# The dense sums of a node group, added in four steps at four successive tiles

## What is computed

```python
h = jnp.einsum('ni,rio->rno', X, W)                  # 4 relations
msg = h[etype, src] * inv_deg[:, None]
agg = jax.ops.segment_sum(msg, dst, num_segments=X.shape[0])
out = agg + X @ root + bias
out = (out - mu) * jax.lax.rsqrt(var + EPS) * gamma + beta
out = jax.nn.elu(out)
return out + X
```

## Time and profile before

| what | value |
|---|---|
| median of 3 runs | 5862.45 us (5860.99 to 5867.11) |
| span of the profiled execution | 5905.4 us |
| PE busy | 4806.4 us, 81% |
| DVE busy | 3711.0 us, 63% |
| POOL busy | 3267.9 us, 55% |
| ACT busy | 1418.0 us, 24% |

### The profile page before, as it was taken

How to read it: one execution, slowest core, us unless ns; L and a number is a source line. 1 busy time by engine, 2 the same in 40 slices (tenths; PEclk the granted TensorE clock), 3 DMA queues, 4 the chain that set the end, 5 groups by cost and what they waited for, 6 DMA issues and landing times.

```text
span 5905.4 us, 80081 instructions
## 1 busy us (share of the span) xinstructions
PE 4806.4 (81%) x20415; PEld 3355.2 (57%) x20415; DVE 3711.0 (63%) x9969; ACT 1418.0 (24%) x3629; POOL 3267.9 (55%) x3256
## 2 busy tenths in 40 slices
PE   5878876777888887888887888887888888777776
PEld 4544432345666665666664666665666665556555
DVE  7998885565666664555554555555556555566665
ACT  1046653213555551111111111111111111011011
POOL 0058871003666664666664666665666664666664
PEclk8999998999999998999998999998999998888888
DMA  1000016312555555555555555555555555444444
GB/s 49 1 1 1 1 21 228 143 61 89 159 156 161 162 158 170 161 157 155 159 157 150 162 156 159 159 155 161 155 158 155 159 159 152 144 143 145 143 140 126
DMA packets 398886, 772.61 MB, mean 131 GB/s; under 512 B 77327, under 2 KB 166113, under 8 KB 398424
## 3 DMA queue, kind: packets, MB, share of 16 engines
q0 software_dynamic: 150720, 386.19, 24.2%
q1 hardware_dynamic: 246824, 380.53, 19.2%
q10 hardware_dynamic: 1008, 1.84, 0.1%
HBM read 652.04 MB, written 115.89 MB: 130 GB/s over the span
## 4 chain that ended last, share of the span: by engine, by line
PE 65%; issue 13%; DVE 12%; another core or an unknown queue 5%; ACT 2%; DVEq 2%; DMA 1%; ACTq 0%; SPq 0%
PE psum L736 24%; PE psum L758 23%; PE psum L690 5%; PE psum L807 3%; DVE arena L1429 3%; PE psum L840 2%; PE psum L793 2%; DVE arena L1571 2%; DVE arena L1303 2%; DVE arena L1290 2%; PE psum L700 1%; DVE arena L1238 1%; PE psum L622 1%; DVE emat L1409 1%
## 5 line engine op out<-in xcount | busy, mean ns | idle before, releaser
L584 POOL DMA_INDIRECT msg<-h_table,g_rel x1880 | 1795.6, 955 | 1088.5 <-issue 419.9
L1429 DVE TENSOR_TENSOR arena<-arena,psum 128x256 f32 x2940 | 1224.7, 417 | 1434.8 <-PE psum L758 970.4
L758 PE MATMUL psum<-msg,emat 128*128 128x256 f32 x4704 | 1519.7, 413 | 547.7 <-issue 323.1
L758 PEld LDWEIGHTS psum<-msg,emat 128*128 128x128 f32 x4704 | 892.9, 202 | 1021.7 <-issue 795.6
L1409 DVE TENSOR_SCALAR emat<-iota,node,weight 128x128 f32<-128x128 f32 x2352 | 862.9, 368 | 139.4 <-issue 58.8
L736 PE MATMUL psum<-arena,emat 128*128 128x256 f32 x3200 | 908.1, 405 | 6.3 <-issue 6.1
L584 POOL DMA_INDIRECT msg<-h_table,g_src x472 | 457.0, 968 | 726.3 <-PE psum L758 591.0
L736 PEld LDWEIGHTS psum<-arena,emat 128*128 128x128 f32 x3200 | 647.5, 204 | 134.0 <-issue 35.5
L566 POOL DMA_INDIRECT placed_rows<-leaving,idx x300 | 439.6, 1465 | 423.3 <-issue 416.7
L584 POOL DMA_INDIRECT hout<-h_table,g_rel x472 | 451.3, 956 | 275.4 <-issue 110.2
L793 PE MATMUL psum<-arena,emat 125*128 125x453 f16 x2000 | 448.0, 358 | 85.9 <-DVE arena L1303 85.9
(11 more groups left out here) (253 smaller groups left out, 5331.1 us busy)
## 6 DMA issues: line engine op xcount, KB each, us to landing
emat<-count_blocks SPq DMA_DIRECT2D x496, 256.0 KB
more_blocks<-count_blocks SPq DMA_DIRECT2D x372, 256.0 KB
count_blocks<-emat SPq DMA_DIRECT2D x200, 256.0 KB
h_table<-hout SPq DMA_DIRECT2D x100, 512.0 KB
msg<-h_table,g_rel POOLq DMA_INDIRECT x1880
arena<-h_table SPq DMA_DIRECT2D x24, 512.0 KB
msg<-h_table,g_src POOLq DMA_INDIRECT x472
hout<-h_table,g_rel POOLq DMA_INDIRECT x472
```

Of the source, the lines that this page charges most:

```text
L584: pool.indirect_dma_start(out=slots[n % RING], out_offset=None, in_=table[:, :], in_offset=bass.IndirectOffsetOnAxis(ap=rows[:, t:t + 1], ...
L758: pe.matmul(agg_ps[n % NPS][:, 0:D], emat[:, n % BODY, :], slots[n % RING], start=True, stop=True).then_inc(s_mm, 1)
L1429: dve.tensor_tensor(a, a, agg_ps[n % NPS][:, 0:D], ALU.add).then_inc(s_acc, 1)
```

## The change

In passes 1 to 4 the four additions of dense sums of a window no longer follow one another. Relation r has the key d - DA + r, so the four stand behind the additions of tiles d-6, d-5, d-4 and d-3. Each addition of the tile behind a step waits for that step (`s_dstep`, and `s_dense` behind the last one). In pass 0 the one addition stays where it is, and the wait for it moves from right behind it to just ahead of the next tile's addition. PE, ACT, POOL and SP execute the same instructions in the same order as before.

```diff
+            dense_step_at = {done_at[j] - DA + r: (j, r) for j in range(NW) for r in range(R)}
+
             def add_tiles(q, work):
...
+                    if t in dense_step_at:
+                        j, r = dense_step_at[t]
+                        if q == 0 and r == 0 or r == R - 1:
+                            dve.wait_ge(s_dense, q * NW + j + 1)
+                        elif q:
+                            dve.wait_ge(s_dstep, ((q - 1) * NW + j) * (R - 1) + r + 1)
                     dve.wait_ge(s_mm, MM0 + n + 1)
...
-            def dense_added(q, j):
+            def dense_begun(q, j):
                 n, v = q * NW + j, window_at(mybir.EngineType.DVE, j)
-                a = cols(acc, v * D, D)
                 dve.wait_ge(s_used, (n + 1) * K)
-                dve.wait_ge(s_acc, ACC0 + q * NT + done_at[j] - DA)
                 if q == 0:
...
+            def dense_added(q, j, r, v):
+                n, a = q * NW + j, cols(acc, v * D, D)
+                dve.wait_ge(s_acc, ACC0 + q * NT + done_at[j] - DA + r)
+                added = dve.scalar_tensor_tensor(
+                    a, dense_ps[r // 2][:, r % 2 * D:(r % 2 + 1) * D],
+                    cols(inv, v + r * NW, 1), a, ALU.mult, ALU.add)
+                if r < R - 1:
+                    added.then_inc(s_dstep, 1)
                 else:
-                    for r in range(R):
...
-                dve.wait_ge(s_dense, n + 1)
+                    added.then_inc(s_dense, 1)
...
                 for j in range(NW):
-                    steps[done_at[j] - DA] = lambda j=j: dense_added(q, j)
+                    for r in range(R if q else 1):
+                        steps[done_at[j] - DA + r] = lambda j=j, r=r: dense_step(j, r)
```

More of the change, by code:

```diff
@@ L1558, in window_work @@
                 return work
-            def dense_added(q, j):
+            def dense_begun(q, j):
                 n, v = q * NW + j, window_at(mybir.EngineType.DVE, j)
-                a = cols(acc, v * D, D)
                 dve.wait_ge(s_used, (n + 1) * K)
-                dve.wait_ge(s_acc, ACC0 + q * NT + done_at[j] - DA)
                 if q == 0:
+                    a = cols(acc, v * D, D)
+                    dve.wait_ge(s_acc, ACC0 + q * NT + done_at[j] - DA)
                     dve.tensor_tensor(a, a, dense_ps[0][:, 0:D], ALU.add).then_inc(s_dense, 1)
-                else:
-                    for r in range(R):
[L1569 to L1574, removed]
-                dve.wait_ge(s_dense, n + 1)
+                return v
+            def dense_added(q, j, r, v):
[6 more added lines that the diff above has]
+                    added.then_inc(s_dstep, 1)
+                else:
+                    added.then_inc(s_dense, 1)
             def window_steps(q):
@@ L1588, in window_steps, with dense_step @@
                 after = sorted(window_work(q, 0, 0) if q else first_work(0, 0))
+                dense_of = {}
+                def dense_step(j, r):
+                    if r == 0:
+                        dense_of[j] = dense_begun(q, j)
+                    if q:
+                        dense_added(q, j, r, dense_of[j])
                 for j in range(NW):
-                    steps[done_at[j] - DA] = lambda j=j: dense_added(q, j)
+                    for r in range(R if q else 1):
+                        steps[done_at[j] - DA + r] = lambda j=j, r=r: dense_step(j, r)
                     for i in after:
```

## The result

The changed kernel takes 5874.02 us (median of 20 runs, 5859.51 to 5889.03), the kernel before, on the same chip, 5863.96 us (median of 20, 5856.70 to 5873.81). The ratio is 1.0018, 95% interval [1.0012, 1.0024]: about 10 us slower, just inside the 0.2% that I had called "same". I had forecast 33 us slower. The direction was right, the size three times too large.

What follows compares the result with a forecast made beforehand. No engine was full; waiting between PE and DVE was taken as the bound. Later dense products cost 43 us in passes 1 to 3, pass 4 0, 10 us given back: +33, 5862 to 5895 us, range 5800 to 5945.

Steps and rivals of the forecast that it cites:

- The stall ahead of tile d-1, up to 1.93 us earlier: PE may start tile d-1 up to 1.93 us earlier per window; taken alone worth at most 193 us.
- The dense product at 5.5 at the earliest, and 1.0 us later in half of the windows: PE's first dense product waits for the fourth step; passes 1 to 3: half the windows 1.0 later, half 0.2, 43 us.
- The late results: PE's results reach DVE later than modelled matmul ends; late case taken for half of 72 windows, start 1.0 us later.
- Pass 4 and pass 0 at nothing: Pass 4's 24 windows cost 0; in pass 0 only the wait of its one addition per window moves: nothing.
- What is given back, 10 us: Less queued on DVE behind the window's end, and PE's tiles d-1 and d done earlier: 10 us taken back.
- The clock, as before: PE's spells at the lower clock, 1.2 GHz, stay as many as before, in pass 4 too.
- DVE's own work at nothing: DVE's work grows one or two tenths of a us per window, covered by idle time: nothing; uncovered, 15 us.
- gain reaches the path: Rival: late windows start the dense product at 5.5, half their low-clock spells go; 5767 full, 5815 half; chance 0.31.
- Nothing in sum: Rival: losing and gaining windows cancel, or the four banks even it out; 5863, within 0.2%; chance 0.18.

Runs made afterwards that it cites:

- the second profile of before: The kernel before, unchanged, profiled once more because its first profiled execution was a long one: span 5856.5 us, time 5858.26 us.
- e5_one_of_four: The kernel before with only the last relation's dense addition in passes 1 to 4, the other three left out: 5848.74 us, ratio 0.9970.
- e13_bank_wait2: The changed kernel, but a window's first two dense products wait only for the second dense addition, the third for the fourth: 5911.11 us, ratio to before 0.9997.
- e15_two_and_two: Half way between the kernel before and the changed one: two dense additions behind tile d-6, two behind tile d-5; 5911.14 us, ratio to before 1.0004.
- e12_changed_again: The changed kernel, unchanged, run again on another chip: 5928.64 us, ratio to the kernel before 1.0032.
- e8_run_at_d2: The kernel before with its run of four dense additions kept whole but three tiles later, behind tile d-3: 5932.36 us, ratio 1.0122.
- e9_half_products: The kernel before without the dense products of relations 1 and 2 in passes 1 to 4, 14 per window in place of 28: 5831.59 us, ratio 0.9934.
- e10_half_gathers: The kernel before, gathering only 64 of a tile's 128 rows in passes 1 to 4: 5869.66 us, ratio 0.9997.

## Why the prediction was right in direction and wrong in size

*The stall ahead of tile d-1, up to 1.93 us earlier.* Right as to the mechanism. Summed over the 100 windows of passes 1 to 4, PE's idle time just ahead of tile d-1 fell from 168 us in the second profile of before to 48. That this is worth less than its length was expected; with it and three quarters of the additions gone `e5_one_of_four` gained 16 us, and in the two versions without a wait (`e13_bank_wait2`, `e15_two_and_two`) it is worth nothing measurable.

*The dense product at 5.5 at the earliest, and 1.0 us later in half of the windows.* Right in its place, right in sum, somewhat wrong in its parts. Over the 72 windows of passes 1 to 3, the first product started 6.19 us behind the addition of tile d-6 in the second profile of before, and 6.68 in the changed kernel: 0.49 x 72 = 35 us, where I had 43 (pass 4, which I had at nothing, adds 6). Starts beyond 7 us were 14 and became 27, so fewer windows had been late than the half I took. The three examples of the earlier trace rows came from an execution with more of them (21). The cycle of a tile and a step is 1.24 and 1.22 us where nothing is late (3407.36, 3408.60 and 3409.82 in DVE's rows above), not 1.40, so that the earliest start is 1.47 + 1.24 + 1.22 + 0.56 + 0.48 + 0.11 = 5.1 rather than 5.5.

*The late results.* The waits stayed: 793.6 us ahead of DVE's additions were put down to PE's matmuls in passes 1 to 4 before, 817.7 after. In DVE's rows above, DVE waits 1.18 us for PE's result of tile d-5, added at 3407.36, though the modelled end of that matmul is at 3401.6 (start 3401.01, duration 0.59). Going by the waits and not by the modelled ends was right: the product did not start at 5.5 nearly everywhere, but at 6.68 in the mean. The Trainium skill, "Perfetto Trace Analysis", section "Tensor Engine Instruction (MATMUL, LD_WEIGHTS)", says that the end of a matmul in a profile is an estimate and not observed, and the trace agrees.

*Pass 4 and pass 0 at nothing.* Right for the time: pass 4 took 870.5 us before and 870.6 after. Its first products did start later, at 6.32 us in place of 6.08, over 24 windows. Pass 0 went from 860.6 to 863.2, which is within what two executions differ by.

*What is given back, 10 us.* This is the term that was mis-sized, and the step that failed: I carried the lateness of the first product into the length of the pass almost in full. Over all 96 windows that have a successor the product was 35 + 6 = 41 us late in sum, close to the 43 of the forecast, but the four passes are only 16.2 us longer, and by the medians of the runs it is 10 us. So 25 to 31 us were given back, not 10. The runs of the second chip show the same more strongly. In `e13_bank_wait2` the first product starts 1.12 us earlier than in `e12_changed_again` in passes 1 to 3 (5.61 against 6.73) and 1.45 earlier in pass 4 (4.58 against 6.03), 115 us in sum, and the passes are 16.3 us shorter. In `e15_two_and_two` it starts 0.40 and 0.26 us earlier (6.33 and 5.77), 35 us in sum, and the kernel is as fast as `e13_bank_wait2`. There is no fixed share of the lateness that reaches the end.

Part of it is given back early. Counted from the addition of tile d-6, that of tile d+3 started at 14.22 us before and 14.45 after in passes 1 to 3, so 0.23 of the 0.49 us are left there. 0.23 x 72 = 17 us would be just what the passes lost, but that may be chance: in pass 4 the same count gives 0.55 us later (13.48 and 14.03), 13 us in sum, and pass 4 is no longer than before. I had reckoned a late product as lost time for the whole queue behind it. But tiles d-1 and d had been done earlier, and both engines had less to make up before they next met. That this is how it was given back is argued, not shown.

*The clock, as before.* Wrong. I summed the stretches below full clock: in passes 1 to 4 they are 516 us in the second profile of before and 569 in the changed kernel; 613 in `e12_changed_again` and 421 in `e13_bank_wait2` beside it. I had expected as many as before; they are fewer (86, where there were 94) and longer. At half speed, 53 us more of them give up to 27 us more busy time of PE, and the rows show 28.4. They lie where the new wait lies: in the 6 us behind the first product of a window, summed over 96 windows, the clock was at the lower level for 174 us before and 227 in the changed kernel, for 243 in `e12_changed_again` and 90 in `e13_bank_wait2`. So products often began at 1.2 GHz before the change too, and the wait made it worse. I had treated a pause of PE as the same wherever it lies.

How much of the loss is the clock's is not shown. `e15_two_and_two` has 563 us at the lower level, 169 of them behind first products, `e13_bank_wait2` 421 and 90, and the two take the same time, 5911.14 and 5911.11 us. The Trainium skill, "TensorE: Matmul & The Clock Gate", section "A second HAM failure mode: psum-queue depth-cycling", says of another kernel that frequent short pauses between groups of matmuls make the clock swing and cost throughput. The trace agrees as to the swings (94 stretches at the lower level before, 86 after); a cost in proportion to the time at the lower level these two runs don't bear out. Whether a late start at full clock would cost anything by itself was not tried.

*DVE's own work at nothing.* Right: its busy time in passes 1 to 4 went from 2055.0 to 2037.5 us, and its idle time ahead of additions grew by 67 us (1131.7 at L1429 to 1198.6 at L1437).

*The rival "gain reaches the path"* fell with `e5_one_of_four` and `e13_bank_wait2`. *"Nothing in sum"* (5863) was, by size, a better forecast than mine (5895): the measured 5874.02 is 11 us from the one and 21 from the other.

**What stays open.** What sets the pace of a pass. PE is busy 737 us in a mean pass and 646 with fewer products, and a pass keeps 859 to 876. No engine fills a pass alone; GpSimd is busy 558 us of it. DVE's waits ahead of tile additions that the profile puts down to PE's tile matmuls, often with a modelled end long past, are its largest idle item with all dense products in place: 778 to 841 us in passes 1 to 4 of the profiles before and after and of `e8_run_at_d2`, `e12_changed_again`, `e13_bank_wait2` and `e15_two_and_two`. In `e9_half_products` this item is 392.3 us, but 613.2 us are put down to "remote" there, another core or an unknown queue, and the sum with the rest, 1135.9 us, is that of the kernel before (1131.7). The traces don't show when a result becomes visible. The gathers as what sets the pace were not tested either, since `e10_half_gathers` took only 84 us from GpSimd. More than four banks for tiles were not tried; the kernel uses the others for dense sums and projections.

## What to carry to other kernels

Before you split a run of work to fill a stall, look for whoever waits for its last piece: the consumer of the first piece gains, the consumer of the last one pays, and a wait split by bank (`e13_bank_wait2`) took the price away at no cost here. Gauge the gain by a run that leaves the work out; where that brings 0.3%, expect no order of it to bring much more. Do not add up how late one instruction starts: 41 us of lateness made 10 to 16 us here, and 115 us less of it gained 16. And compare PE's busy time as well as its idle time: the wait just ahead of the dense products went with slower products (417 to 431 ns against 402 to 412 where there was no wait).

## What the runs showed of the hardware

- Less idle time of PE went with a longer time, twice: 12 us less and 16 us longer in the changed kernel, 49 us more and 16 us shorter in `e13_bank_wait2` against `e12_changed_again`.
- The time that PE spends at the lower clock level did not order the times by itself: 421 us of it in `e13_bank_wait2` and 563 in `e15_two_and_two` went with 5911.11 and 5911.14 us.
- With 363 us of PE's busy time taken away, the remaining tile matmuls ran at 450 ns instead of 413, with the granted clock at 0.86 to 0.88 instead of 0.94 to 0.95 in passes 1 to 3.
- An indirect gather of 64 rows keeps GpSimd busy nearly as long as one of 128: 3187.2 against 3271.4 us over the program, or 919 ns for one gather in passes 1 to 4 against 955.
- A VectorE TENSOR_SCALAR of 128x8 took 313 ns where 128x128 takes 368.
- Two of the chips used differ by 0.8% with the same program: 5863.96 us and 5911.18 us for the kernel before.
